# Two layer normalisations of an attention tile moved from VectorE to ScalarE, with the statistics in another order

## What is computed

```python
def _layernorm(x, axis=-1, eps=1e-05):
    m = jnp.mean(x, axis=axis, keepdims=True)
    v = jnp.var(x, axis=axis, keepdims=True)
    return (x - m) / jnp.sqrt(v + eps)
...
x = x + jnp.tanh(g_xattn[l]) * xattn_l(_layernorm(x), ctx_768, ...)
x = x + jnp.tanh(g_ffn[l]) * ffn_l(_layernorm(x), ...)
```

## Time and profile before

| | |
|---|---|
| median of 3 runs | 1381.53 us (1380.48 to 1381.85) |
| span of the profiled execution | 1377.6 us |
| PE busy | 1280.6 us, 93% |
| DVE busy | 1069.2 us, 78% |
| ACT busy | 630.4 us, 46% |
| POOL busy | 568.4 us, 41% |

### The profile page before, as it was taken

The page is one execution under the profiler, slowest core; times in us unless marked ns, Lnnn a source line. Parts: engine busy times, 40 slices in busy tenths (PEclk is TensorE's granted clock), DMA queues, the critical chain, the costliest instruction groups (busy, mean ns, idle before and its releaser), DMA issues.

```text
span 1377.6 us, 26563 instructions
## 1 busy us (share of the span) xinstructions
PE 1280.6 (93%) x7754; PEld 948.6 (69%) x7754; DVE 1069.2 (78%) x2395; ACT 630.4 (46%) x1304; POOL 568.4 (41%) x978
## 2 busy tenths in 40 slices
PE   7999699899999799999999998899999999999863
PEld 5666488566666688886676766788888576666612
DVE  4999764799999577777777776677777888888777
ACT  3555342455555522224555554522223555555375
POOL 2666521466666301132544544110101566666413
PEclk9999999999999999999999999999999999999965
DMA  9000200000000200000000000000000000000002
GB/s 231 19 0 1 54 1 0 1 1 0 0 0 1 54 1 0 0 0 1 1 0 0 0 1 1 1 1 0 0 0 1 1 1 0 0 0 1 1 0 61
DMA packets 25465, 15.10 MB, mean 11 GB/s; under 512 B 4574, under 2 KB 24444, under 8 KB 25404
## 3 DMA queue, kind: packets, MB, share of 16 engines
q1 hardware_dynamic: 25404, 14.33, 4.1%
HBM read 12.22 MB, written 2.10 MB: 10 GB/s over the span
## 4 chain that ended last, share of the span: by engine, by line
PE 75%; DVE 5%; ACT 4%; issue 4%; POOL 2%; ACTq 0%; DVEq 0%; POOLq 0%
PE S L1305 29%; PE OX L1305 14%; PE PT L1305 13%; PE GV L1305 11%; PE PT L1467 5%; ACT pT L761 1%; PE OX L1415 1%; POOL arena L558 1%; PE OX L1418 1%; DVE arena L1248 1%; DVE zsum L1001 1%; ACT moe_flat L884 0%; DVE xn L966 0%; POOL x L655 0%; DVE rb L1027 0%
## 5 line engine op out<-in xcount | busy, mean ns | idle before, releaser
L1305 PEld LDWEIGHTS OX<-arena,pT 128*128 128x128 f32 x1792 | 210.9, 192 | 55.2 <-issue 32.9
L558 POOL TENSOR_TENSOR arena<-arena,zinv 128x1024 f32<-128x1024 f32 (+1 forms) x128 | 215.7, 1685 | 78.6 <-DVE zinv L1005 78.5
L1305 PE MATMUL OX<-arena,pT 128*128 128x128 f32 x1792 | 231.4, 281 | 9.6 <-ACT pT L761 6.8
L819 ACT ACTIVATE arena<-S 128x512 f32<-128x512 f32 x144 | 86.0, 597 | 236.6 <-PE S L1305 236.6
L985 DVE TENSOR_REDUCE nmax<-S 128x16 f32<-128x1024 f32 (+1 forms) x128 | 139.7, 1091 | 45.4 <-PE S L1305 38.0
L1148 DVE TENSOR_TENSOR arena<-S,arena 128x512 f32<-128x512 f32 x144 | 99.6, 692 | 86.2 <-ACT arena L819 83.0
L1156 DVE SCALAR_TENSOR_TENSOR x<-PT,gate,x 128x128 f32 (+1 forms) x576 | 161.0, 343 | 2.2 <-PE PT L1305 2.2
L1305 PE MATMUL S<-arena,xT 128*128 (+1 forms) x320 | 160.4, 599 | 1.1 <-ACT arena L741 0.8
L530 POOL TENSOR_TENSOR rstd<-mv,eps 128x1 f32<-128x1 f32 x128 | 24.3, 190 | 312.7 <-DVE mv L987 312.6
L1305 PE MATMUL S<-xh,w_low 128*128 (+1 forms) x320 | 140.4, 439 | 7.2 <-issue 7.2
L994 DVE TENSOR_TENSOR arena<-S,nmax 128x1024 f32<-128x1024 f32 (+1 forms) x128 | 138.1, 1079 | 0.0
(11 more groups left out here) (261 smaller groups left out, 2271.9 us busy)
## 6 DMA issues: line engine op xcount, KB each, us to landing
x<-in_x SPq DMA_DIRECT2D x4, 512.0 KB, 7.0
out<-x SPq DMA_DIRECT2D x8, 256.0 KB, 2.3
moe_flat<-in_L_ffn_w SPq DMA_DIRECT2D x3, 512.0 KB, 6.9
arena<-in_L_xattn_Wq SPq DMA_DIRECT2D x2, 512.0 KB
wo_in<-in_L_xattn_Wo SPq DMA_DIRECT2D x2, 512.0 KB
moe<-in_L_ffn_we_gate SPq DMA_DIRECT2D x1, 512.0 KB, 4.5
moe<-in_L_ffn_we_up SPq DMA_DIRECT2D x1, 512.0 KB, 5.9
moe<-in_L_ffn_we_down SPq DMA_DIRECT2D x1, 512.0 KB, 6.2
```

The lines of the kernel that those rows point to most:

```text
L558: pool.tensor_tensor(pr, pr, z, ALU.mult).then_inc(s.probs_done, 1)
L819: act.activation(silu[:, e % 2, :], S[0][:, BANK * (e % 2):BANK * (e % 2) + BANK], ACT.Silu).then_inc(s.silu_done, 1)
L1305: return pe.matmul(out, lhsT, rhs, start=start, stop=stop)
```

## The change

Both normalisations leave VectorE. ScalarE makes them as an Identity activation, x times a scale per row plus an offset per row: the scale is rstd, the offset -mean times rstd. The offset (shift, shift2) is made by GpSimd in two operations of 128x1: the mean times -1, which needs the statistics only, and that times rstd, after the power. In ScalarE's step the second norm of t-2 stands first, ahead of the exponential, and the first norm of t+4 last. On VectorE bn_stats of t-1 moves behind the maximum and the first bn_aggr, the subtraction waits for it, and the second bn_aggr moves behind the subtraction. Waits are added: GpSimd's on xn_done and xn2_done of four tiles before, VectorE's on shift_done and shift2_done of earlier tiles.

```diff
@@ POOL, attention step: first norm of t+4
                         done(pool, s.mv_done, a.tile0 + n)
+                        done(pool, s.xn_done, a.tile0 + n - 4)
                         pool.tensor_tensor(rstd[:, j, 0:1], mv[:, j, 1:2], eps[:, :], ALU.add).then_inc(s.rstd_step, 1)
+                        pool.tensor_tensor(shift[:, j:j + 1], mv[:, j, 0:1], neg_one[:, :], ALU.mult).then_inc(s.mean_negated, 1)
                         pool.wait_ge(s.rstd_step, steps_of_layer + per * n + 1)
...
+                        pool.wait_ge(s.mean_negated, a.tile0 + n + 1)
+                        pool.wait_ge(s.rstd_done, a.tile0 + n + 1)
+                        pool.tensor_tensor(shift[:, j:j + 1], shift[:, j:j + 1], rstd[:, j, 1:2], ALU.mult).then_inc(s.shift_done, 1)
@@ POOL: second norm of t-1
                         done(pool, s.mv2_done, a.tile0 + n)
+                        done(pool, s.xn2_done, a.tile0 + n - 4)
                         pool.tensor_tensor(rstd2[:, q, 0:1], mv2[:, q, 1:2], eps[:, :], ALU.add).then_inc(s.rstd2_step, 1)
+                        pool.tensor_tensor(shift2[:, q:q + 1], mv2[:, q, 0:1], neg_one[:, :], ALU.mult).then_inc(s.mean2_negated, 1)
                         pool.wait_ge(s.rstd2_step, a.tile0 + n + 1)
                         pool.tensor_tensor(rstd2[:, q, 1:2], rstd2[:, q, 0:1], neg_half[:, :], ALU.pow).then_inc(s.rstd2_done, 1)
+                        pool.wait_ge(s.mean2_negated, a.tile0 + n + 1)
+                        pool.wait_ge(s.rstd2_done, a.tile0 + n + 1)
+                        pool.tensor_tensor(shift2[:, q:q + 1], shift2[:, q:q + 1], rstd2[:, q, 1:2], ALU.mult).then_inc(s.shift2_done, 1)
@@ ACT, attention step
+                def normalised(out, n, j, scale, bias, sm):
+                    act.activation(out, x[:, ds(n, 1), :].rearrange("p a d -> p (a d)"), ACT.Identity,
+                                   scale=scale, bias=bias[:, j:j + 1]).then_inc(sm, 1)
+
                 def step(t, r, i, between=None):
+                    if is_tile(t - 2):
+                        T, q = a.tile0 + t - 2, (r + 2) % 4
+                        act.wait_ge(s.shift2_done, T + 1)
+                        done(act, s.xT2_done, T - 2)
+                        if a.l == 3:
+                            done(act, s.amax_x_done, t - 4)
+                        normalised(xn2[:, r % 2, :], t - 2, q, rstd2[:, q, 1:2], shift2, s.xn2_done)
...
+                    n = t + 4
+                    if is_tile(n):
+                        T = a.tile0 + n
+                        act.wait_ge(s.shift_done, T + 1)
+                        done(act, s.xT_done, T - 2)
+                        normalised(xn[:, r % 2, :], n, r, rstd[:, r, 1:2], shift, s.xn_done)
@@ DVE, attention step
                         dve.wait_ge(s.x_done, a.tile0 + t)
-                    if is_tile(t - 2):
-                        T, q = a.tile0 + t - 2, (r + 2) % 4
-                        done(dve, s.xT2_done, T - 2)
-                        dve.wait_ge(s.rstd2_done, T + 1)
-                        dve.tensor_scalar(xn2[:, r % 2, :], tokens(t - 2), mv2[:, q, 0:1],
-                                          rstd2[:, q, 1:2], ALU.subtract, ALU.mult).then_inc(s.xn2_done, 1)
...
-                    if is_tile(t - 1):
-                        dve.bn_stats(stats2[:, (r + 3) % 4, :], xt).then_inc(s.stats2_done, 1)
-
                     if is_tile(t + 4):
                         dve.wait_ge(s.stats_done, a.tile0 + t + 5)
+                        done(dve, s.shift_done, a.tile0 + t)
                     if is_tile(t - 1):
-                        dve.wait_ge(s.stats2_done, a.tile0 + t)
+                        done(dve, s.shift2_done, a.tile0 + t - 5)
...
                     if is_tile(t - 1):
-                        dve.bn_aggr(mv2[:, (r + 3) % 4, :], stats2[:, (r + 3) % 4, :]).then_inc(s.mv2_done, 1)
+                        dve.bn_stats(stats2[:, (r + 3) % 4, :], xt).then_inc(s.stats2_done, 1)
+                        dve.wait_ge(s.stats2_done, a.tile0 + t)
...
+                    if is_tile(t - 1):
+                        dve.bn_aggr(mv2[:, (r + 3) % 4, :], stats2[:, (r + 3) % 4, :]).then_inc(s.mv2_done, 1)
...
-                        dve.tensor_scalar(xn[:, r % 2, :], tokens(n), mv[:, r, 0:1],
-                                          rstd[:, r, 1:2], ALU.subtract, ALU.mult).then_inc(s.xn_done, 1)
```

More of the change, by code:

```diff
@@ L114, in __init__ @@
         self.xn_done = sem("xn_done")
+        self.shift_done = sem("shift_done")
+        self.mean_negated = sem("mean_negated")
+        self.mean2_negated = sem("mean2_negated")
+        self.shift2_done = sem("shift2_done")
         self.xT_done = sem("xT_done")
@@ L298, in flamingo_program @@
         neg_half = sb("neg_half", [P, 1])
+        neg_one = sb("neg_one", [P, 1])
         eps = sb("eps", [P, 1])
@@ L324, in flamingo_program @@
         rstd2 = sb("rstd2", [P, 4, 2])
+        shift = sb("shift", [P, 4])
+        shift2 = sb("shift2", [P, 4])
         xn2 = sb("xn2", [P, 2, D])
@@ L497, in _ @@
             pool.memset(eps[:, :], EPS).then_inc(s.consts_made, 1)
+            pool.memset(neg_one[:, :], -1.0).then_inc(s.consts_made, 1)
             pool.memset(magic[:, :], MAGIC).then_inc(s.consts_made, 1)
```

7 lines of the change are left out of this document (1 added, 6 removed).

## The result

The changed kernel took 1387.99 us in the median (1385.0 to 1391.21, 9 runs), the kernel before 1381.53 (1378.82 to 1385.2, 9 runs). The ratio is 1.0047, with a 95% interval from 1.0033 to 1.0061: 0.47%, 6.5 us slower. The profiled execution's span is 1384.3 us against 1377.6, and its own time 1386.27, so 2.0 us lie around the span. The 3.9 us that the prediction took for it were the median less the span of one execution that was faster than the median.

A forecast was written before the change was run, and what follows sets the result against it. It took TensorE to bound layers 1 to 3 and VectorE layer 0. Terms -1.3 + 2.2 + 0.75 + 0.55 + 1.0 = +3.2 us on 1377.6 gave 1380.8, plus 3.9 around the span: 1384.7 us, range 1377.0 to 1391.0.

The forecast's parts named there:

- What bounds layers 1 to 3: TensorE is full in these layers' steady stretches, so taking the normalisations' 116.6 us from VectorE gains nearly nothing there.
- Layer 0, steady: Layer 0's steady tiles fall from 3.875 to 3.83 us, 28 tiles by 0.045: -1.3 us.
- the ring over GpSimd's block: Layer 0: two-step wait chain through maximum, GpSimd's block, turning and scores; 7.65 us after the change, 3.83 a step.
- The bound for it (3.95 to 4.0): Layer 0's slower period if dependent steps cost more semaphore delay or rstd2 waits for its aggregate: +2 to +3.5 us.
- That the ring is hidden today, at 3.56 us a step: Layer 0 before the change: the two-step wait chain sums to 7.12 us, hidden under VectorE's 3.875 us a step.
- Layer 1, steady: ScalarE's two Identities take 0.81 us against 0.71 slack, delaying 14 odd steps by 0.16 us: +2.2 us.
- Layers 2 and 3: Steady stretches there neither gain nor lose, since slack covers ScalarE's Identities and GpSimd's 0.5 us longer block.
- Drains and ends: Last steps of each layer's attention lengthen: drains +0.55 us, last normalisations and copies on ScalarE +1.0 us.
- the drain's -0.2: Layer 3's drain gets 0.2 us shorter because a long second normalisation leaves VectorE's chain.
- the end's +0.25: Each layer's end is 0.25 us later, as ScalarE makes both the last Identity and the xT2 copy.
- Starts of the layers: The first normalised tile comes 0.39 us later in layer 0, 0.12 in each other layer: +0.75 us.
- Case B: Rival: layer 0 falls toward 3.6 us, ScalarE's work is hidden; 1375 to 1378 us, chance 0.22.

The follow-up runs named there:

- second_only: The changed kernel with only the second norm moved to ScalarE, the first kept on VectorE, two of GpSimd's four offset operations: 1388.92 us, ratio 1.007 to the kernel before.
- before_pool: The kernel before, norms still on VectorE, with GpSimd's four offset operations added and their result unused: 1396.78 us, ratio 1.0118.
- layers_1_to_3: The change made in layers 1 to 3 alone, layer 0 as in the kernel before: 1385.06 us, ratio 1.0025.
- The second profiles: The changed kernel and the kernel before, each profiled once more unaltered to check TensorE's clock: 1392.28 and 1384.88 us, one run each.
- no_shift_early: The changed kernel without GpSimd's offset operations (constant instead), VectorE's second aggregate directly behind the second statistics: 1380.12 us, ratio 0.9987 to the kernel before.

## Why the prediction came out as it did

The direction and the range (1377.0 to 1391.0) held, with 1387.99 measured for 1384.7: the forecast gave half of the loss. That it fell inside the range is in part luck. Layer 0 was forecast to gain and lost, layer 1 lost less than forecast, and a loss behind layer 2 had no term. Term by term:

- **What bounds layers 1 to 3**: right. VectorE's busy time fell by 138 us (the text said some 160) and gave nothing where TensorE is full.
- **Layer 0, steady: the step that failed.** -1.3 us was forecast, +2.7 us measured between first and last maximum. The mechanism was the right one, the ring over GpSimd's block took VectorE's place, and the block's sizes were off: 2.24 us for 2.10, since the product with rstd starts 99.44 - 98.75 = 0.69 us behind its power, not 0.63, and S to maximum takes 1.15 us for 1.09. A third term was taken wrongly: the mean of 2.59 and 2.40 us from a turning to the next scores. A ring over two steps meets the same kind of step each time, always V or always G, and the longer one sets the pace. In the changed kernel, from the product of 96.83 us on, over a step that fills V:

```profile
97.92 0.66 PE L1489 MATMUL PT<-ident,arena 128*128 128x128 f32 x4 [0.21 <-POOL arena L576]
100.51 1.02 PE L1327 MATMUL S<-arena,xT 128*128 x2
101.67 0.69 DVE L1012 TENSOR_REDUCE nmax<-S 128x8 f32<-128x512 f32 x1 [0.36 <-PE S L1327]
104.77 1.04 POOL L576 TENSOR_TENSOR arena<-arena,zinv 128x512 f32<-128x512 f32 x1
```

 These are 1.09 + 2.59 + 1.16 + 3.10 = 7.94 us, 3.97 each, for the 3.965 measured; with the mean of 2.50 they would be 3.93. A gain of 0.045 us a tile was a difference between two sums of five rows each, and less than their errors. The bound for it (3.95 to 4.0) stood in the text, with two reasons. One, the aggregate behind the subtraction, holds the second norm's sum back by itself (second_only), but not the period: the order without the offset gave 3.77 to 3.79.
- **That the ring is hidden today, at 3.56 us a step**: wrong. It closes over TensorE's output and VectorE's work ahead of the maximum, which the prediction left out. The kernel before, with the turning of 106.09 us of the earlier trace rows between the second and the third row:

```profile
102.56 0.69 DVE L985 TENSOR_REDUCE nmax<-S 128x8 f32<-128x512 f32 x1
105.00 1.04 POOL L558 TENSOR_TENSOR arena<-arena,zinv 128x512 f32<-128x512 f32 x1
107.69 1.16 PE L1305 MATMUL OX<-arena,pT 128*128 128x128 f32 x8
109.00 0.29 DVE L955 TENSOR_TENSOR x<-OX,x 128x128 f32 x1
110.40 0.69 DVE L985 TENSOR_REDUCE nmax<-S 128x8 f32<-128x512 f32 x1
```

 The output ends at 108.85 and the addition starts 0.15 us later; from maximum to maximum it is 7.84 us here and 2 x 3.875 = 7.75 in the mean. VectorE's own work and this ring thus stand close to the same period. before_pool shows that the ring binds. There the product started 3.17 us behind the maximum instead of 2.43, 0.74 us later, and the tile took 0.36 us longer, half of it: the whole delay came through, two steps to a ring, so the ring stood at the period of 3.875 already. By the prediction's ring, 3.56 + 0.27 = 3.83, it would have stayed hidden. The change escapes a part of it by taking the second norm out of this ring.
- **Layer 1, steady**: the size was off. ScalarE's pair takes 332.03 - 331.26 = 0.77 us in an odd step of the changed kernel, so with the slack of 0.71 it would cost 0.06 us in such a step, not 0.16; measured were 0.45 us over 20 tiles, for 2.2 over 28 in the forecast. The copy of xT in odd steps does follow the exponential without idle time, as forecast, but the weight loads' wait for pT became no longer (4.3 us in 18 waits between 295 and 435 us, before 4.9), so it isn't shown that the pair causes the 0.45 us. The order of the statistics alone cost 1.23 us there with the norms on VectorE, and layers_1_to_3, with the changed kernel's code in this layer, 1.03.
- **Layers 2 and 3**: nothing in layer 2, as said; 0.45 us over 20 tiles in layer 3, which the order of the statistics alone gives as well; it was not costed there.
- **Drains and ends**: +0.55 and +1.0 us were forecast. From the last maximum to the last copy of xT2 the four layers took 12.55, 17.54, 17.38 and 18.27 us before and 13.56, 18.07, 17.96 and 18.97 after: 2.8 us in all, for 1.55. The second profiles give 1.8, with up to 1.35 us between the two profiles of one kernel in a single layer. Layer 1's last copies, before and after, against the earlier trace rows:

```profile
465.99 0.28 ACT L725 ACTIVATE ra<-OX 128x128 f32<-128x128 f32 x1 [0.68 <-PE OX L1418]
```

```profile
466.92 0.49 ACT L722 ACTIVATE xn<-x,shift,rstd 128x128 f32<-128x128 f32 x1 [0.57 <-POOL shift L570]
...
468.56 0.28 ACT L754 ACTIVATE ra<-OX 128x128 f32<-128x128 f32 x1 [0.64 <-PE OX L1440]
```

 The copy of the last tile starts 18.1 us behind the last maximum (450.5) for 17.5 (448.4). In layer 3 the drain's -0.2 and the end's +0.25 would leave nothing; both pairs of profiles show +0.7.
- **TensorE's clock**: no term at all. The text ahead of the prediction calls the clock full in all but the last slices of the page, but a slice shows 9 for 90% or more, and the row from 861 to 891 us has 0.89 in the kernel before. Behind layer 2 the clock stood at its lower level for some 10 us more in the changed kernel, and the way to layer 3 took 3.4 us more, the largest single loss outside layer 0. That it goes with the offset is what the table's profiles show, with the reserve said there; how the offset brings it about is open.
- **Starts of the layers** (+0.75): not to be told from the clock's variation at the layers' edges.
- **The rule on the shared ports**, which the prediction took from the Trainium skill (SBUF — State Buffer, section SBUF: two separate sides), agreed with the row and was of no worth for the time. Case B needed layer 0 to fall toward 3.6; with VectorE freed in no_shift_early it still stood at 3.77, on 1/sum.

What isn't settled: the entries of the table of stretches add up to 7.1 us for two profiles each, with opposite entries of 1 us that no experiment explains, and layers_1_to_3 with its interval of 1.5 to 5.4 us holds either share.
